# Layer norm of a macaron layer: statistics of the next tile ahead of the current one's finish, loads moved behind it

## The chip, the cores and the metric

The program runs on all 8 cores of one Trainium2 chip. Each core does its own share and none waits for another. The metric is the time on the device of the slowest core, in microseconds (us).

## The reference, cut to what matters

```python
# x: (4, 4096, 2048) float32
x = x + 0.5 * ffn(layernorm(x))     # 2048 -> 8192 -> 2048, 8-bit weights with scales
x = x + attn(layernorm(x))          # chunked gated linear attention
x = x + 0.5 * ffn(layernorm(x))     # the same weights again

def layernorm(x, eps=1e-5):         # over the 2048 features, no gain or bias
    m = mean(x, -1); v = var(x, -1)
    return (x - m) / sqrt(v + eps)
```

## The kernel before, in words

A core owns 2048 rows (tokens) of x and takes 256 rows ahead of them as a prefix: 2304 rows, 18 tiles of 128 rows. The phases follow one another with barriers between them: layer norm 1 with the gate and up products (pG), the down product (pD), layer norm 2 with the key, query and gate products (pKq, pWg), the scan, the output products (pGo), layer norm 3 with gate and up again (16 tiles), and the down product.

All three layer norms are one Python generator in `ln_transpose`, which emits one tile per step. In this text a tile's number is `ti`, and its steps are:

- **Load.** `xload(ti)` issues one DMA of 1 MiB from ScalarE's queue (ACT) into one of two buffers lnx, `ti % 2`. It must wait until the tile two before it in that buffer has been read by the square and by the normalization.
- **Statistics.** VectorE (DVE) sums the tile (L261); ACT squares it with a running sum, L263. The squares themselves are thrown away; they land in the buffer lnxn of that tile, of which there are three (two in layer norm 2).
- **Finish.** Three small DVE operations (L267, L270, L273) make mean and variance, two small ACT operations (Ln L277, Exp L281) the inverse root, one more small one (L284) the offset, and L287 writes the normalized tile in bf16 to lnxn.
- **Transpose.** TensorE (PE) transposes 16 blocks in two halves (L297); ACT copies the first half out of PSUM (L303), DVE the second (L309). In layer norm 2 the tile is also written to HBM (xn2tok) by a DMA from GpSimd's queue (POOL).

In the code before, step `ti` is: issue load `ti + 1`, statistics of `ti`, finish of `ti`, transpose of `ti`. Load 0 is issued when the generator is made, ahead of everything else in the phase.

Every engine runs its instructions in the order in which they were emitted, and a DMA issued from ACT stands in ACT's order like any other instruction. Semaphore waits are put in by a helper that knows the last writer and the readers of each buffer.

The steps are drawn in groups by `drive`: four tiles, then the products that need these 512 rows, then the next four. With 18 tiles the groups are 4, 4, 4, 4 and 2, with 16 tiles four of 4. In the feed-forward phases a group is followed by ten products (five gate, five up blocks) whose evacuations are ACT's Silu (L405) and a DVE operation (L411). Before the first group, ten weight blocks (wraw) are loaded by SyncE's queue (SP) and converted on ACT (L375). In layer norm 2 a group is followed by the key product, and after the third and fifth group also by query products, softmax and the pWg pass; its first group comes right after the issue of four loads of s_wqk from POOL's queue.

Of the kernel before, what the change touches and what calls it, by code (L numbers as in the profile page):

```python
# [11 lines left out]
AF = mybir.ActivationFunctionType  # L12
ALU = mybir.AluOpType
AX = mybir.AxisListType
# [147 lines left out]
def uname(base):  # L162
    _uid[0] += 1
    return f"{base}_{_uid[0]}"


def build_program(T_OWN, T_PRE, stop=99, scan_stop=99):
# [35 lines left out]
    with ExitStack() as ctx:  # L203
        em = Em(nc, ctx)
# [17 lines left out]
        def ln_transpose(al, srcs, xnT, bxnT, TT_loc, tok_dst=None,  # L222
                         nxn=3):
            if True:
                a2 = al
                pT = [a2(nc.psum_tensor(uname("pT"), [128, 1024], BF16))
                      for _ in range(2)]
                bpT = [Buf(uname("bpT"), excl=True) for _ in range(2)]
                s_x = [a2(nc.sbuf_tensor(uname("lnx"), [128, H], F32))
                       for _ in range(2)]  # L230
                s_xn = [a2(nc.sbuf_tensor(uname("lnxn"), [128, H], BF16))
                        for _ in range(nxn)]
                s_st = a2(nc.sbuf_tensor(uname("lnst"), [128, 24], F32))
                bx = [Buf("lnx0"), Buf("lnx1")]
                bxn = [Buf(uname("lnxn")) for _ in range(3)]
                bstl = [Buf(uname("lnst")) for _ in range(3)]
                bsql = [Buf(uname("lnsq")) for _ in range(3)]
                xnT3 = xnT[:, :].rearrange("p (h t) -> p h t", t=TT_loc)
                tiles = []
                for (src, row0, ntiles) in srcs:  # L240
                    for kk in range(ntiles):
                        tiles.append(src[row0 + kk * 128: row0 + (kk + 1) * 128, :])

                def xload(ti):
                    em.dma("dA", s_x[ti % 2][:, :], tiles[ti],
                           writes=[bx[ti % 2]])

                xload(0)

                def _gen():  # L250
                    for ti in range(len(tiles)):
                        sl = ti % nxn
                        c0 = sl * 8
                        X, BX = s_x[ti % 2], bx[ti % 2]
                        XN, BXN = s_xn[sl], bxn[sl]
                        bst = bstl[sl]
                        st = s_st[:, c0:c0 + 8]
                        if ti + 1 < len(tiles):
                            xload(ti + 1)
                        bsq = bsql[sl]  # L260
                        em.op("dve", lambda v: v.reduce_sum(  # L261
                            st[:, 0:1], X[:, :], AX.X), reads=[BX], writes=[bst])
                        em.op("act", lambda a: a.activation(  # L263
                            XN[:, :], X[:, :], AF.Square,
                            accum_out=st[:, 1:2]),
                            reads=[BX], writes=[BXN, bsq])
                        em.op("dve", lambda v: v.tensor_scalar(  # L267
                            st[:, 2:3], st[:, 0:1], 1.0 / H, None, ALU.mult),
                            reads=[bst], writes=[bst])
                        em.op("dve", lambda v: v.tensor_tensor(  # L270
                            st[:, 3:4], st[:, 2:3], st[:, 2:3], ALU.mult),
                            reads=[bst], writes=[bst])
                        em.op("dve", lambda v: v.scalar_tensor_tensor(  # L273
                            st[:, 4:5], st[:, 1:2], 1.0 / H, st[:, 3:4],
                            ALU.mult, ALU.subtract), reads=[bst, bsq],
                            writes=[bst])
                        em.op("act", lambda a: a.activation(  # L277
                            st[:, 5:6], st[:, 4:5], AF.Ln,
                            bias=s_cst[:, 0:1]),
                            reads=[bst, b_c], writes=[bst])  # L280
                        em.op("act", lambda a: a.activation(  # L281
                            st[:, 6:7], st[:, 5:6], AF.Exp, scale=-0.5),
                            reads=[bst], writes=[bst])
                        em.op("dve", lambda v: v.scalar_tensor_tensor(  # L284
                            st[:, 7:8], st[:, 2:3], -1.0, st[:, 6:7],
                            ALU.mult, ALU.mult), reads=[bst], writes=[bst])
                        em.op("dve", lambda v: v.tensor_scalar(  # L287
                            XN[:, :], X[:, :], st[:, 6:7], st[:, 7:8],
                            ALU.mult, ALU.add), reads=[BX, bst], writes=[BXN])
                        if tok_dst is not None:  # L290
                            em.dma("dV", tok_dst[ti], XN[:, :], reads=[BXN])
                        for half in range(2):
                            pb = bpT[half]
                            em.dep_wait("pe", [BXN, b_c], [pb])
                            for hh in range(8):
                                hc = half * 8 + hh
                                ins = nc.tensor.transpose(  # L297
                                    pT[half][:, hh * 128:(hh + 1) * 128],
                                    XN[:, hc * 128:(hc + 1) * 128], s_ident[:, :])
                                if hh == 7:  # L300
                                    em._finish(ins, "pe", 1, [BXN, b_c], [pb])
                            if half == 0:
                                em.op("act", lambda a, ti=ti: a.activation(  # L303
                                    xnT3[:, 0:8, ti * 128:(ti + 1) * 128],
                                    pT[0][:, :].rearrange(
                                        "p (h t) -> p h t", t=128),
                                    AF.Copy), reads=[pb], writes=[bxnT[ti]])
                            else:
                                em.op("dve", lambda v, ti=ti: v.tensor_copy(  # L309
                                    xnT3[:, 8:16, ti * 128:(ti + 1) * 128],  # L310
                                    pT[1][:, :].rearrange(
                                        "p (h t) -> p h t", t=128)),
                                    reads=[pb], writes=[bxnT[ti]])
                        yield ti
                return _gen()

        def drive(gen, done, need):
# [256 lines left out]
        with ExitStack() as ph:  # L574
            alP = ph.enter_context
            xnT = alP(nc.sbuf_tensor("xn1T", [128, NH * TT], BF16))
            bxnT = [Buf(f"xn1T{i}") for i in range(nT)]
            ln_srcs = ([(dx_pre, 0, nPre)] if nPre else []) + [(dx_own, 0, nTo)]
            g_ln = ln_transpose(alP, ln_srcs, xnT, bxnT, TT)
            if stop <= 1:  # L580
                drain(g_ln)
                em.drain_dmas()
                return nc
            ffn_gu(alP, xnT, bxnT, TT, True, ln_gen=g_ln)
# [11 lines left out]
        with ExitStack() as ph:  # L596
# [18 lines left out]
            with ExitStack() as ps:  # L615
                a2 = ps.enter_context
                g_ln = ln_transpose(a2, [(dx1, 0, nT)], xnT, bxnT, TT,
                                    tok_dst=dxn2, nxn=2)
                if stop <= 4:
# [23 lines left out]
                for wi, wsrc_ap in enumerate((dwq, dwk)):  # L643
                    w3 = wsrc_ap.rearrange("(h p) d -> p h d", p=128)
                    for part in range(2):
# [5 lines left out]
                               writes=[b_wqk])  # L651
# [88 lines left out]
                for ng, (o, wd) in enumerate(groups):  # L740
# [5 lines left out]
                        reads=[pbuf], writes=[b_kf])  # L746
# [19 lines left out]
            with ExitStack() as ps:  # L766
# [235 lines left out]
                for po in range(nTo):  # L1002
                    sl = po % 2
# [6 lines left out]
                    for dvc in range(NH):  # L1010
# [9 lines left out]
                        reads=[bpR, b_c], writes=[b_rr])  # L1020
# [3 lines left out]
                        reads=[b_rr], writes=[b_rr])  # L1024
# [8 lines left out]
            for cc in range(NH):  # L1033
                em.dma("dV", s_wo[:, cc * H:(cc + 1) * H], dwbfa[2, cc],
                       writes=[b_wo])
            with ExitStack() as ps:
# [4 lines left out]
                for (o, wd) in tgroups(T_OWN):  # L1041
# [3 lines left out]
                        writes=[b_pGo[0]])  # L1045
                    em.op("dve", lambda v, o=o, wd=wd: v.tensor_copy(
                        s_rb[:, o:o + wd], pGo[:, 0:wd]),
                        reads=[b_pGo[0]], writes=[b_rb])
# [20 lines left out]
                for c in range(T_OWN // SW):  # L1069
                    for cb in range(NH):  # L1070
# [3 lines left out]
                        for g2 in range(SW // 512):  # L1074
# [3 lines left out]
                                   writes=[b_gwi[slw]])  # L1078
                        g0 = (2 * cb) % 4
                        for g2 in range(SW // 512):  # L1080
# [14 lines left out]
                              reads=gbk + [b_gwi[slw]],  # L1095
                              writes=[b_gof])
                        em.op("act", lambda a: a.activation(
                            s_sg[:, 0:SW], s_gof[:, 0:SW], AF.Silu),
                            reads=[b_gof], writes=[b_sg])
# [8 lines left out]
                              reads=[b_o, b_rb, b_c], writes=[b_gof])  # L1108
# [3 lines left out]
                            reads=[b_gof, b_sg], writes=[b_yb])  # L1112
                    for sub in range(SW // 128):
# [3 lines left out]
                               writes=[b_xr2])  # L1117
                        for half in range(2):
                            bk = [b_pGo[2 * half], b_pGo[2 * half + 1]]
                            em.dep_wait("pe", [b_yb, b_wo], bk)  # L1120
                            for cc in range(NH):
                                for tg in range(2):
# [18 lines left out]
                                  reads=bk + [b_xr2], writes=[b_xo2])  # L1141
# [89 lines left out]
```

How the kernel before makes its waits and increments, by code:

```python
    def _wait(self, ename, sem_name, val):  # L56
        if val <= 0:
            return
        w = self.waited[ename]
        if w.get(sem_name, 0) >= val:
            return
        self.eng[ename].wait_ge(self.sem[sem_name], val)
        w[sem_name] = val
# [19 lines left out]
    def _finish(self, ins, sem_name, inc, reads, writes):  # L83
        ins.then_inc(self.sem[sem_name], inc)
        self.cnt[sem_name] += inc
        tag = (sem_name, self.cnt[sem_name])
        for b in writes:
            b.last_w = tag
            b.readers = []
        for b in reads:
            b.readers.append(tag)
        return ins
```

## Time and profile before

| what | value |
|---|---|
| median of three runs | 7669.69 us (7666.61 to 7678.71) |
| the profiled execution: its time / its span | 7678.08 us / 7676.6 us |
| spans of the eight cores | 7647.7 to 7676.6 us |
| PE matmul busy | 6659.8 us (87%) |
| ACT busy / DVE busy / POOL busy | 1545.2 (20%) / 1142.9 (15%) / 281.3 us (4%) |
| DMA engines, mean rate | 83 GB/s |
| layer norm tiles per core | 52 (18 + 18 + 16) |

The profile is of the slowest core, core 3. Its span runs from its first to its last instruction. A bracket at the end of a line of the timeline gives how long the engine had been idle, and what ended that; ACTq, SPq and POOLq are the issues of DMAs from that engine. The granted clock is the share of TensorE's full clock that it was given.

### The profile page before, as it was taken

Reading aid. Unit: us, or ns where it says so; the run is one execution under the profiler, and the core shown is the slowest. Engines: PE = TensorE matmul, PEld = TensorE weight load, DVE = VectorE, ACT = ScalarE, POOL = GpSimd, SP = SyncE. Lnnn points to the kernel's source line nnn. Section 1 sums busy time; section 2 is a strip of 40 time slices with the busy share of each in tenths; the row PEclk is TensorE's granted clock in tenths of the full one; section 3 lists DMA queues with packets and bytes.
Section 4 is the critical chain, followed back from the end, with each engine's and each line's share of the span. In section 5 each row is a group of like instructions: output and inputs, shape, how many; then the busy total and the mean of one; then the engine's idle time right before and its main releaser. Section 6 shows DMA issues by size and latency. Waiting matters only on the chain.

```text
span 7676.6 us, 80477 instructions; the slowest of 8 cores (7647.7 to 7676.6 us)
## 1 busy us (share of the span) xinstructions
PE 6659.8 (87%) x32377; PEld 3176.0 (41%) x32377; DVE 1142.9 (15%) x1540; ACT 1545.2 (20%) x1518; POOL 281.3 (4%) x366
## 2 busy tenths in 40 slices
PE   4599999999978989966656995599999999889899
PEld 1245555555543434433334342244444444334344
DVE  2211111111100000022143331211111111000000
ACT  2232222222221020012223002222222222210200
POOL 0000000000000000000000000000000000000000
PEclk8799999999999999977877997799999999999999
DMA  2133333222124444442212433111111111144444
GB/s 67 44 88 90 85 91 85 85 90 83 38 55 132 115 124 115 115 126 97 101 53 66 137 116 99 55 42 38 38 39 39 39 39 39 55 132 115 125 114 107
DMA packets 743465, 635.59 MB, mean 83 GB/s; under 512 B 581952, under 2 KB 623040, under 8 KB 730048
## 3 DMA queue, kind: packets, MB, share of 16 engines
q10 hardware_dynamic: 590208, 257.98, 12.8%
q1 hardware_dynamic: 102304, 196.28, 8.5%
q0 software_dynamic: 50592, 176.18, 7.8%
q8 instruction: 267, 4.37, 0.2%
q14 instruction: 94, 0.77, 0.0%
HBM read 464.69 MB, written 166.72 MB: 82 GB/s over the span
## 4 chain that ended last, share of the span: by engine, by line
PE 84%; DVE 5%; ACT 5%; DMA 3%; issue 3%; DVEq 0%; ACTq 0%; SPq 0%; POOL 0%; POOLq 0%
PE pG L127 50%; PE pD L545 24%; PE pWg L127 3%; PE pGo L1123 3%; ACT wdsb L524 2%; PE pGo L127 2%; DVE lnst L261 1%; DMA gwi<-gwig 1%; DVE lnxn L287 1%; PE pT L297 1%; PE pKq L127 1%; DVE s_S L968 1%; ACT silu L405 0%; PE pOs L916 0%; DVE hsb L411 0%
## 5 line engine op out<-in xcount | busy, mean ns | idle before, releaser
L545 PE MATMUL pD<-wdsb,hts 128*128 128x512 bf16 x8704 | 1889.0, 380 | 203.7 <-DMA hts<-h4s 203.7
L127 PE MATMUL pG<-xn1T,wbf 128*128 128x512 bf16 (+1 forms) x10240 | 2014.7, 360 | 49.8 <-ACT silu L405 23.9
L127 PE MATMUL pG<-xn3T,wbf 128*128 128x512 bf16 x8192 | 1789.5, 381 | 47.9 <-ACT silu L405 23.7
L127 PEld LDWEIGHTS pG<-xn1T,wbf 128*128 128x128 bf16 x10240 | 1003.4, 98 | 1060.1 <-issue 87.3
L545 PEld LDWEIGHTS pD<-wdsb,hts 128*128 128x128 bf16 x8704 | 853.7, 98 | 1238.8 <-issue 218.4
L127 PEld LDWEIGHTS pG<-xn3T,wbf 128*128 128x128 bf16 x8192 | 802.5, 98 | 1034.0 <-issue 85.4
L405 ACT ACTIVATE silu<-pG,s_gs 128x512 bf16<-128x512 f32 (+1 forms) x576 | 382.1, 663 | 2879.8 <-PE pG L127 2879.7
L411 DVE SCALAR_TENSOR_TENSOR hsb<-pG,s_us,silu 128x512 bf16<-128x512 f32 (+1 forms) x576 | 415.4, 721 | 3484.9 <-PE pG L127 3479.3
L375 ACT ACTIVATE wbf<-wraw 128x2048 bf16<-128x2048 uint8 x256 | 478.8, 1899 | 140.9 <-DMA wraw<-wg 139.1
L297 PE MATMUL pT<-s_ident,lnxn 128*128 128x128 bf16 x832 | 97.0, 310 | 469.8 <-DVE lnxn L287 469.8
L524 ACT ACTIVATE wdsb<-wdu 128x8192 bf16<-128x8192 uint8 x32 | 222.0, 7015 | 961.5 <-issue 900.8
L560 DVE TENSOR_TENSOR t<-pD,dsbl 128x1024 f32<-128x1024 f32 x68 | 83.3, 1225 | 1913.6 <-PE pD L545 1913.6
L113 POOL DMA_DIRECT2D h4s<-hsb x128 | 152.6, 1192 | 4104.8 <-DVE hsb L411 4104.8
L297 PEld LDWEIGHTS pT<-s_ident,lnxn 128*128 128x128 bf16 x832 | 84.7, 144 | 484.8 <-issue 484.8
L1123 PE MATMUL pGo<-s_wo,s_yb 128*128 128x512 bf16 x1024 | 224.1, 382 | 15.8 <-DVE s_yb L1109 15.4
L127 PE MATMUL pGo<-s_o,s_wb 128*128 128x512 bf16 x1024 | 226.4, 383 | 10.4 <-DVE s_gof L1091 9.3
L127 PE MATMUL pWg<-xn2T,wigb 128*128 128x512 bf16 x1024 | 226.1, 385 | 0.0
L263 ACT ACTIVATE lnxn<-lnx 128x2048 bf16<-128x2048 f32 x52 | 98.9, 1902 | 521.1 <-DMA lnx<-x1s 512.5
L1123 PEld LDWEIGHTS pGo<-s_wo,s_yb 128*128 128x128 bf16 x1024 | 100.6, 98 | 139.4 <-issue 20.9
L127 PEld LDWEIGHTS pGo<-s_o,s_wb 128*128 128x128 bf16 x1024 | 100.3, 99 | 137.4 <-issue 21.0
L127 PEld LDWEIGHTS pWg<-xn2T,wigb 128*128 128x128 bf16 x1024 | 101.3, 99 | 124.1 <-issue 6.3
L261 DVE TENSOR_REDUCE lnst<-lnx 128x1 f32<-128x2048 f32 x52 | 118.3, 2276 | 28.3 <-DMA lnx<-x2s 14.4
(110 smaller groups left out, 1564.2 us busy)
## 6 DMA issues: line engine op xcount, KB each, us to landing
hts<-h4s ACTq DMA_DIRECT2D x272, 512.0 KB, 3.9
h4s<-hsb POOLq DMA_DIRECT2D x64, 576.0 KB, 5.4
wraw<-wg SPq DMA_DIRECT2D x128, 256.0 KB, 2.6
wraw<-wu SPq DMA_DIRECT2D x128, 256.0 KB, 2.7
wdu<-wd SPq DMA_DIRECT2D x32, 1024.0 KB, 5.3
h4s<-hsb POOLq DMA_DIRECT2D x64, 512.0 KB, 4.8
wbfa<-cab POOLq DMA_DIRECT2D x48, 512.0 KB, 5.5
x1s<-xo POOLq DMA_DIRECT2D x36, 512.0 KB, 3.8
```

The lines of the kernel that those rows point to most:

```text
L113: ins = self.eng[ename].dma_start(out_ap, in_ap)
L127: ins = self.nc.tensor.matmul(out_ap, l, r, start=(k == 0), stop=last)
L261: em.op("dve", lambda v: v.reduce_sum(st[:, 0:1], X[:, :], AX.X), reads=[BX], writes=[bst])
L263: em.op("act", lambda a: a.activation(XN[:, :], X[:, :], AF.Square, accum_out=st[:, 1:2]), reads=[BX], writes=[BXN, bsq])
L297: ins = nc.tensor.transpose(pT[half][:, hh * 128:(hh + 1) * 128], XN[:, hc * 128:(hc + 1) * 128], s_ident[:, :])
L375: em.op("act", lambda a: a.activation(WB[:, :], WR[:, :], AF.Copy, bias=-128.0), reads=[BWR], writes=[BWB])
L405: em.op("act", lambda a: a.activation(SL[:, o:o + wd], pap, AF.Silu, scale=scale2[:, ib:ib + 1]), reads=[pbuf, b_c], writes=[BSL])
L411: em.op("dve", lambda v: v.scalar_tensor_tensor(HT[:, o:o + wd], pap, scale2[:, ib:ib + 1], SL[:, o:o + wd], ALU.mult, ALU.mult), reads=[p ...
L524: em.op("act", lambda a, c8=c8: a.activation(s_wd[:, c8 * 8 * HH:(c8 + 1) * 8 * HH], s_wdu8[c8 % 2][:, :], AF.Copy, bias=-128.0), reads=[b ...
L545: last_ins = nc.tensor.matmul(pD[sl][:, tg * 512:(tg + 1) * 512], HB[:, il * 128:(il + 1) * 128], s_wd[:, ic * HH + tg * 512: ic * HH + (t ...
L560: em.op("dve", lambda v, sl=sl, half=half: v.tensor_tensor(s_t1[sl][:, :], pD[sl][:, :], s_dsb[:, half * HH:(half + 1) * HH], ALU.mult), r ...
L1123: ins = nc.tensor.matmul(pGo[:, half * 1024 + tg * 512: half * 1024 + (tg + 1) * 512], s_yb[:, cc * SW + sub * 128: cc * SW + sub * 128 + ...
```

## The change

Inside the generator the statistics of a tile become a function `head`, and the order changes. Loads 0 and 1 and the statistics of tile 0 are emitted at the generator's first step, no longer when it is made. Step `ti` then is: statistics of `ti + 1`, finish of `ti`, transpose of `ti`, issue of load `ti + 2`. Buffers, their number, and the work done stay as they were.

```diff
-                xload(0)
+                def head(tj):
+                    slh = tj % nxn
+                    sth = s_st[:, slh * 8:slh * 8 + 8]
+                    Xh, BXh = s_x[tj % 2], bx[tj % 2]
+                    XNh, BXNh = s_xn[slh], bxn[slh]
+                    em.op("dve", lambda v: v.reduce_sum(
+                        sth[:, 0:1], Xh[:, :], AX.X), reads=[BXh],
+                        writes=[bstl[slh]])
+                    em.op("act", lambda a: a.activation(
+                        XNh[:, :], Xh[:, :], AF.Square,
+                        accum_out=sth[:, 1:2]),
+                        reads=[BXh], writes=[BXNh, bsql[slh]])
 
                 def _gen():
+                    xload(0)
+                    if len(tiles) > 1:
+                        xload(1)
+                    head(0)
                     for ti in range(len(tiles)):
...
                         if ti + 1 < len(tiles):
-                            xload(ti + 1)
-                        bsq = bsql[sl]
-                        em.op("dve", lambda v: v.reduce_sum(
-                            st[:, 0:1], X[:, :], AX.X), reads=[BX], writes=[bst])
-                        em.op("act", lambda a: a.activation(
-                            XN[:, :], X[:, :], AF.Square,
-                            accum_out=st[:, 1:2]),
-                            reads=[BX], writes=[BXN, bsq])
+                            head(ti + 1)
...
+                        if ti + 2 < len(tiles):
+                            xload(ti + 2)
                         yield ti
```

## Rows read from the trace of the kernel before

**Rows 1.** The page: chain that ended last by line, and the transposes' group.
```profile
PE pG L127 50%; PE pD L545 24%; PE pWg L127 3%; PE pGo L1123 3%; ACT wdsb L524 2%; PE pGo L127 2%; DVE lnst L261 1%; DMA gwi<-gwig 1%; DVE lnxn L287 1%; PE pT L297 1%; PE pKq L127 1%; DVE s_S L968 1%; ACT silu L405 0%; PE pOs L916 0%; DVE hsb L411 0%
...
L297 PE MATMUL pT<-s_ident,lnxn 128*128 128x128 bf16 x832 | 97.0, 310 | 469.8 <-DVE lnxn L287 469.8
```

**Rows 2.** Windows: length, busy us of PE, PEld, DVE, ACT, POOL, PE clock, DMA.
```profile
122.00:163.00 41.00, 11.15 (x81) 8.12 (x82) 20.20 (x29) 14.99 (x22) 0.00 (x0) 0.61 0.29 103
```

**Rows 3.** Timeline, two neighbouring tiles of layer norm 1: start, us, instruction [idle before].
```profile
52.71 1.35 DVE L287 TENSOR_SCALAR lnxn<-lnx,lnst 128x2048 bf16<-128x2048 f32 x1
...
54.42 1.87 PE L297 MATMUL pT<-s_ident,lnxn 128*128 128x128 bf16 x16 [6.87 <-DVE lnxn L287]
...
55.60 0.34 ACTq L113 DMA_DIRECT2D lnx<-x_own  x1
...
56.65 0.69 DVE L309 COPY xn1T<-pT 128x1024 bf16<-128x1024 bf16 x1 [2.60 <-ACT xn1T L303]
57.26 2.27 DVE L261 TENSOR_REDUCE lnst<-lnx 128x1 f32<-128x2048 f32 x1
...
60.48 0.29 ACT L277 ACTIVATE lnst<-lnst,s_cst 128x1 f32<-128x1 f32 x1 [2.05 <-DVE lnst L273]
...
61.44 1.35 DVE L287 TENSOR_SCALAR lnxn<-lnx,lnst 128x2048 bf16<-128x2048 f32 x1
```

**Rows 4.** DMA issues of lnx by stretch: count, KB, median us to landing; last, all 52.
```profile
lnx<-x_own ACTq DMA_DIRECT2D x13, 1024.0 KB, 5.0
...
lnx<-x1s ACTq DMA_DIRECT2D x13, 1024.0 KB, 5.5
...
lnx<-x2s ACTq DMA_DIRECT2D x14, 1024.0 KB, 4.8
...
lnx<-x1s ACTq DMA_DIRECT2D x1, 1024.0 KB, 7.7
...
DMA to landing us min/median/max: 4.7/5.2/12.1
```

**Rows 5.** DMA issues at the program's start; the load is the second one.
```profile
s_ident<-ident SPq DMA_DIRECT2D x1, 32.0 KB, 4.6
...
s_gs<-gs SPq DMA_DIRECT2D x1, 32.0 KB, 1.8
...
lnx<-x_pre ACTq DMA_DIRECT2D x1, 1024.0 KB, 6.6
```

**Rows 6.** Timeline, layer norm 1: issue of load 1, normalization of tile 0.
```profile
39.08 0.34 ACTq L113 DMA_DIRECT2D lnx<-x_pre  x1
...
44.19 1.35 DVE L287 TENSOR_SCALAR lnxn<-lnx,lnst 128x2048 bf16<-128x2048 f32 x1
```

**Rows 7.** Timeline, layer norm 2: writes 0 and 1, square 2, key product.
```profile
3403.46 1.10 POOL L113 DMA_DIRECT2D xn2tok<-lnxn  x2
...
3410.93 1.91 ACT L263 ACTIVATE lnxn<-lnx 128x2048 bf16<-128x2048 f32 x1 [8.55 <-DMA xn2tok<-lnxn]
...
3427.75 5.54 PE L127 MATMUL pKq<-xn2T,s_wqk 128*128 128x512 bf16 x16 [1.21 <-DVE xn2T L309]
```

**Rows 8.** Timeline, layer norm 3: issues of loads 0 and 1, normalization of tile 0.
```profile
4669.32 0.36 ACTq L113 DMA_DIRECT2D lnx<-x2s  x1
...
4699.65 0.33 ACTq L113 DMA_DIRECT2D lnx<-x2s  x1
...
4706.04 1.35 DVE L287 TENSOR_SCALAR lnxn<-lnx,lnst 128x2048 bf16<-128x2048 f32 x1
```

**Rows 9.** DMA issues of wraw: the first of phase 3, then all 128.
```profile
wraw<-wg SPq DMA_DIRECT2D x1, 256.0 KB, 7.1
...
wraw<-wg SPq DMA_DIRECT2D x128, 256.0 KB, 2.6
```

**Rows 10.** The chain in order of time: first product after two of the groups.
```profile
251.27 6.58 PE pG L127 x16
...
339.81 5.00 PE pG L127 x16
```

More of the change, by code:

```diff
@@ L257, in _gen @@
                         st = s_st[:, c0:c0 + 8]
+                        bsq = bsql[sl]
                         if ti + 1 < len(tiles):
-                            xload(ti + 1)
-                        bsq = bsql[sl]
-                        em.op("dve", lambda v: v.reduce_sum(
-                            st[:, 0:1], X[:, :], AX.X), reads=[BX], writes=[bst])
-                        em.op("act", lambda a: a.activation(
-                            XN[:, :], X[:, :], AF.Square,
-                            accum_out=st[:, 1:2]),
-                            reads=[BX], writes=[BXN, bsq])
+                            head(ti + 1)
                         em.op("dve", lambda v: v.tensor_scalar(
```

## The prediction, on record before the result

> **What bounds the kernel now.** I read the page's shares and chain first. The chain is PE nearly throughout, and the layer norm has three entries of about 1% in it, the sum L261, the normalization L287 and the transposes [rows 1]. The transposes' row says more: PE sat idle 469.8 us ahead of them, 9.0 us for each of 52 tiles, every time ended by L287 [rows 1]. So the layer norm is exposed, tile by tile, and nothing else runs on PE meanwhile: in the stretch of the second group PE is busy 11.15 us of 41, most of that products at its two ends [rows 2]. What one tile takes longer, the kernel takes longer.
>
> The timeline of two neighbouring tiles gives the cycle [rows 3]. L287 starts at 52.71 and again at 61.44: a period of 8.73 us. Within it, counted from the end of L287 at 54.06: PE starts at +0.36, the next load is issued at +1.54, DVE copies its half at +2.59, and the next sum starts at +3.20. From the start of the sum to the next L287 it is 4.18 us. The load is not in this loop: the one issued at +1.54 is for the tile after the next, so it has 1.66 us plus a whole period, 10.4 us, before anyone reads it, and it takes 4.8 to 5.5 us [rows 4].
>
> **The change, part by part.**
>
> *Statistics one tile ahead: nothing gained in the middle.* DVE runs in order. Before, its order is sum(i), small ones(i), L287(i), copy(i), sum(i+1). After, it is sum(i+1), small ones(i), L287(i), copy(i), sum(i+2). There is still one full sum between copy and the next small ones, so it covers none of DVE's idle gaps (2.60 us ahead of the copy [rows 3]). ACT's square lies beside the sum as before. Price and gain: 0 per tile. Only a layer norm's last tile has no statistics in its step: 2.27 us saved [rows 3], three times: -6.8.
>
> *The load behind the finish: its cover is gone.* Load i+2 is issued at the end of step i, which is the same point of the cycle as before, +1.54. But the next instruction on both DVE and ACT is now the statistics of this very tile i+2, and the finish of tile i+1, whose data are long there, is queued behind them on both engines; PE waits for that finish. So the sum starts at +1.54, plus the landing, plus 0.1 for the wait to pass (my allowance), in place of +3.20. With the medians of the three layer norms [rows 4]:
> - layer norm 1: 1.54 + 5.0 + 0.1 - 3.20 = 3.44 us more per stall;
> - layer norm 2: with 5.5, 3.94 us;
> - layer norm 3: with 4.8, 3.24 us.
>
> To hide the load it would have to land within 1.56 us; the fastest of all 52 took 4.7 [rows 4].
>
> *How many stalls.* The load issued at a group's end flies during the products, so the group's first step does not wait. The other three steps of a group of four do, also the fourth, which takes the statistics of the next group's first tile before its own finish. The last group's last step has no statistics, and a group of two has no stall. That makes 3+3+3+3+0 = 12 for layer norm 1, as many for layer norm 2, and 3+3+3+2 = 11 for layer norm 3.
> - Layer norm 1: 12 x 3.44 = 41.3.
> - Layer norm 2 without its first group: 9 x 3.94 = 35.5.
> - Layer norm 3: 11 x 3.24 = 35.6.
> Together 112.4 us for 32 stalls. Bounds: with 4.7 for each, 32 x 3.14 = 100; with 7.7 (the slowest load late in layer norm 2 [rows 4]) for the nine of layer norm 2 and 5.4, my guess from the medians, for the others, 9 x 6.14 + 23 x 3.84 = 144.
>
> The Trainium skill, page "DMA: Bandwidth & Descriptors", section on the anatomy of one DMA, puts a transfer at about 2.0 us plus bytes over 436 GB/s, fitted for DMAs issued by GpSimd. For 1 MiB that is 4.4 us, an estimate; by it a stall would be 2.8 us and the 32 of them 91 us. The trace has 4.7 to 5.5 for loads issued by ACT in the steady part, so the sum goes by the trace. By the page too, the fixed 2.0 us alone exceed the room there is.
>
> *First group of layer norm 2.* There the third tile already waits: square 2 overwrites lnxn 0, whose write to HBM stands on POOL's queue behind the s_wqk loads, is issued at 3403.46, and lets the square go at 3410.93 [rows 7]. From there to the key product it is 16.8 us. After the change the same square stands ahead of the finish of tile 1. The later start of tile 0 is hidden in this wait. From the square: 2.1 us of it and its accumulator read, 1.0 from Ln to L287(1) [rows 3], then two stalled periods of 8.73 + 3.94 = 12.67, then 4.8 from L287(3) to the product (16.8 less 8.73 and less the 3.3 from square to L287): 33.2 us, 16.4 more. The write may land up to 2.4 us sooner when it no longer shares with write 1, so 14.0 to 16.4; I take 15.5.
>
> *The starts.* In layer norm 1 load 0 is now issued behind the ten conversions, with load 1 right behind it, where load 1 is issued today at 39.08 [rows 6]. That place took 6.6 us for one load [rows 5]; a second one behind it lands, I estimate, 3.7 later: less than the 4.7 of the fastest load, since what is fixed in a load overlaps. (Where two are issued together now, in layer norm 2, the second takes 12.1 [rows 4].) Sum 1 then starts at 39.1 + 10.4 = 49.5, and L287 of tile 0 at 53.7 instead of 44.19: +9.5. Against it, load 0 no longer competes with the small constants at the front: s_ident took 4.6 us, s_gs of the same size 1.8 [rows 5], and each waits for the one before it and the weights for all of them. I credit 2.5 of at most some 3.4: +7.0. In layer norm 3 the first wraw took 7.1 us beside load 0 and 2.6 otherwise [rows 8, 9], so the conversions move up by at most 4.5; I take 4.0. Loads 0 and 1 then go at 4695.7, the second lands about 9.2 later, L287 follows 4.2 after the sum's start and 1.3 for the table load that Ln needs there: 4710.5 against 4706.04 [rows 8], +4.5. Both starts +11.5, between +6 and +18.
>
> *The clock.* The layer norms run at the low clock already, 0.61 granted over that stretch [rows 2], so longer gaps have little left to take. The first product after a group takes 6.58 us in some and 5.00 in others [rows 10]. Of the eight such products with 512 columns in the two feed-forward phases six are like the first of these rows, each with a second slow product behind it, and the difference over both is 3.3 us. A new draw could give back 20 or cost 7; I take 0.
>
> *Sum:* 112.4 + 15.5 + 11.5 - 6.8 = +132.6 us. Against the profiled execution's own time, 7678.1, that is 7810.7; it lies 8.4 above the median of the runs shown, so against the median, which I forecast, 7802.
>
> **Rivals.**
> - *The sum comes out of the loop* (ends on the other side). Statistics a tile ahead are to take 2.3 us off each tile. It holds if DVE finds the sum ready to run in its idle gap; 49 x 2.4 = -118 us, 7552. DVE's 2.60 us gap speaks for it. In-order issue behind the load of the same tile speaks against it, and it decides only if loads land within 1.56 us.
> - *No change.* The stall is just hidden, at a landing near 1.6 us: 7670. All 52 landings speak against it.
> - *Partly hidden.* Some finishes slip through, or half of the stalls in a group are shorter since the queue is emptier: about half the stalls, 7745. For it: layer norm 2 has other waits already. Against it: the layer norms have nothing else on the queues in phases 1 and 3.
> - *Dearer.* Loads on the path see contention or the clock costs after every group: 32 stalls at 6.1 instead of 3.5, +216 in all, 7886. Only the load late in layer norm 2 speaks for it.
>
> **How the numbers follow.** The forecast's case gets 0.83, partly hidden 0.07, dearer 0.05, faster 0.03, no change 0.02. Its range, all ends low: 100 + 14 + 6 - 7 - 20 = +93, all high: 144 + 16 + 18 - 7 + 7 = +178. I take 7768 to 7848 as the range. A change under 0.2%, 15 us, is about what a measurement of this kernel cannot tell from none. Faster 0.03, same 0.02, slower 0.95.
>
> **What would show it.** In the profile after: a period near 12.2 us within a group and 8.7 for its first tile; the sum L261 and the square L263 in 35 places with an idle time ended by the DMA of lnx, 3 to 4 us beyond what they idle now; PE's idle time before the transposes near 600 us instead of 469.8; s_ident landing in about 2 us; the products as they were. The prediction is wrong if sums start right behind the copies, or if loads land in clearly less than 4.7 or more than 6 us.

## The result, and the profile after

The changed kernel takes 1.0166 times as long as before (95% interval 1.0150 to 1.0182): 7669.7 becomes some 7797 us, +127. The prediction was 7802. Some executions leave the four cores of a die, or all eight, at a lower granted clock (down to 0.78, where the others have 0.925 to 0.94) and take longer, so where an experiment is compared below, its number is the mean span of the cores over those dies alone whose granted clock lies within 0.004 of the highest of that kernel: 7660 us for the kernel before (single dies 7656 to 7667), 7784 for the changed one (7780 to 7800), +124.

The page of the changed kernel, first from the costliest groups (busy, mean ns of one, idle before and its releaser), then the DMA issues with their median us to landing, over the whole execution:

```profile
L306 PE MATMUL pT<-s_ident,lnxn 128*128 128x128 bf16 x832 | 97.0, 309 | 586.8 <-DVE lnxn L296 586.8
...
L253 DVE TENSOR_REDUCE lnst<-lnx 128x1 f32<-128x2048 f32 x52 | 118.8, 2284 | 220.4 <-DMA lnx<-x1s 72.8
```
```profile
lnx<-x1s ACTq DMA_DIRECT2D x18, 1024.0 KB, 5.4
lnx<-x_own ACTq DMA_DIRECT2D x16, 1024.0 KB, 4.9
lnx<-x2s ACTq DMA_DIRECT2D x16, 1024.0 KB, 4.8
...
s_ident<-ident SPq DMA_DIRECT2D x1, 32.0 KB, 2.7
```

PE's idle time ahead of the transposes grew from 469.8 [rows 1] to 586.8 us, by 117, which is nearly all of the loss. The loads themselves land as before (4.8 to 5.4 against 4.8 to 5.5 [rows 4]); they are only waited for now. The timeline of two neighbouring tiles of layer norm 1, to be laid beside [rows 3], shows where (L296 is the normalization that was L287, L253 the sum that was L261, L256 the square, L318 DVE's copy):

```profile
63.14 1.35 DVE L296 TENSOR_SCALAR lnxn<-lnx,lnst 128x2048 bf16<-128x2048 f32 x1
64.85 1.87 PE L306 MATMUL pT<-s_ident,lnxn 128*128 128x128 bf16 x16 [9.91 <-DVE lnxn L296]
...
66.03 0.33 ACTq L113 DMA_DIRECT2D lnx<-x_own  x1
67.09 0.69 DVE L318 COPY xn1T<-pT 128x1024 bf16<-128x1024 bf16 x1 [2.60 <-ACT xn1T L312]
70.92 1.91 ACT L256 ACTIVATE lnxn<-lnx 128x2048 bf16<-128x2048 f32 x1 [3.94 <-DMA lnx<-x_own]
70.93 2.29 DVE L253 TENSOR_REDUCE lnst<-lnx 128x1 f32<-128x2048 f32 x1 [3.15 <-DMA lnx<-x_own]
...
75.17 1.35 DVE L296 TENSOR_SCALAR lnxn<-lnx,lnst 128x2048 bf16<-128x2048 f32 x1
```

Up to the copy the cycle is the same to a hundredth: the load is issued 1.54 us after L296's end, the copy starts at 2.60. Then DVE and ACT idle until the load issued a moment ago has landed, 4.9 us after its issue. The square that ends this wait belongs to the tile after the next; the tile whose transposes PE is waiting for had its data all along. L296 to L296 is 12.03 us here instead of 8.73.

The stages, as means over the eight cores of one profiled execution (layer norms 1 and 2 with the products among their groups; the third from the end of pWg to its last copy). In that of the changed kernel cores 4 to 7 took 15 us more than cores 0 to 3 (7800.1 against 7785.3), so its row is some 7 us high:

| kernel | LN 1 | FFN 1 | LN 2 | scan, pGo, LN 3 | FFN 2 | all |
|---|---|---|---|---|---|---|
| before | 402.0 | 2967.4 | 497.5 | 1116.9 | 2678.2 | 7662.1 |
| changed | 448.4 | 2968.2 | 539.4 | 1154.2 | 2682.6 | 7792.7 |
| statistics in place, load late | 443.9 | 2968.2 | 545.6 | 1154.8 | 2676.7 | 7789.2 |
| changed, three lnx buffers in LN 1 and 3 | 402.7 | 2967.4 | 539.7 | 1117.4 | 2679.7 | 7707.0 |
| changed, loads 0 and 1 early | 442.3 | 2967.6 | 539.7 | 1149.6 | 2677.9 | 7777.0 |
| statistics in the gaps, ACT's queue | 366.6 | 2968.2 | 476.4 | 1085.2 | 2679.6 | 7576.0 |

### The profile page after: what moved, and what is told of

It reads as the page before. It is cut to its first block, busy times and chain, and to the rows that moved or that the text cites. A ratio compares the mean times of both kernels' runs of the same rounds, so it can differ in the third digit from the quotient of the medians.

```text
span 7810.0 us, 80408 instructions; the slowest of 8 cores (7773.6 to 7810.0 us)
## 1 busy us (share of the span) xinstructions
PE 6669.3 (85%) x32377; PEld 3178.2 (41%) x32377; DVE 1142.0 (15%) x1540; ACT 1550.1 (20%) x1518; POOL 280.4 (4%) x366
## 4 chain that ended last, share of the span: by engine, by line
PE 82%; DMA 6%; DVE 5%; ACT 4%; issue 3%; DVEq 0%; ACTq 0%; POOL 0%; SPq 0%; POOLq 0%
PE pG L127 49%; PE pD L556 24%; PE pGo L1134 3%; PE pWg L127 3%; ACT wdsb L535 2%; PE pGo L127 2%; DVE lnst L253 1%; DMA gwi<-gwig 1%; DVE lnxn L296 1%; DMA lnx<-x1s 1%; DMA lnx<-x_own 1%; DMA lnx<-x2s 1%; PE pT L306 1%; DMA wdu<-wd 1%; DVE s_S L979 1%
## 5 line engine op out<-in xcount | busy, mean ns | idle before, releaser
L306 PE MATMUL pT<-s_ident,lnxn 128*128 128x128 bf16 x832 | 97.0, 309 | 586.8 <-DVE lnxn L296 586.8
L256 ACT ACTIVATE lnxn<-lnx 128x2048 bf16<-128x2048 f32 x52 | 99.2, 1907 | 682.8 <-DMA lnx<-x1s 562.9
L253 DVE TENSOR_REDUCE lnst<-lnx 128x1 f32<-128x2048 f32 x52 | 118.8, 2284 | 220.4 <-DMA lnx<-x1s 72.8
```

The costliest lines, as they stand in the source:

```text
L253: em.op("dve", lambda v: v.reduce_sum(sth[:, 0:1], Xh[:, :], AX.X), reads=[BXh], writes=[bstl[slh]])
L256: em.op("act", lambda a: a.activation(XNh[:, :], Xh[:, :], AF.Square, accum_out=sth[:, 1:2]), reads=[BXh], writes=[BXNh, bsql[slh]])
L306: ins = nc.tensor.transpose(pT[half][:, hh * 128:(hh + 1) * 128], XN[:, hc * 128:(hc + 1) * 128], s_ident[:, :])
```

## The experiments

**The late load alone.** The order of the statistics is that of the kernel before; only the load moves.

```diff
-                        if ti + 1 < len(tiles):
-                            xload(ti + 1)
                         bsq = bsql[sl]
...
+                        if ti + 1 < len(tiles):
+                            xload(ti + 1)
                         yield ti
```

> The kernel before with one thing changed: the load of tile i+1 is issued at the end of step i instead of at its start; statistics stay in their old place. Theory (the price is a load whose landing the in-order engines wait for): the period within a group goes from 8.73 to about 12.0 us, in 13 + 12 places of layer norms 1 and 3 and 9 or 10 of layer norm 2 plus its first group; 35 x 3.3 = 115, with the first group some +120 us in all, ratio 1.015 to 1.017. Rival (the statistics ahead of the finish are what costs): the order of DVE and ACT work is that of before, so within 0.2% of before.

Measured: 7792 us, +132, slightly more than the change itself. There is no later start of layer norm 1 in it (tile 0 is normalized at 43.9 us in the mean of the eight cores, before at 43.7), but each layer norm's last step is stalled too: 11.8, 14.4 and 11.9 us where the kernel before has 8.5, 8.7 and 8.7. From its timeline in layer norm 1 (L285 is the normalization, L261 the square):

```profile
57.62 1.35 DVE L285 TENSOR_SCALAR lnxn<-lnx,lnst 128x2048 bf16<-128x2048 f32 x1
59.33 1.86 PE L295 MATMUL pT<-s_ident,lnxn 128*128 128x128 bf16 x16 [11.21 <-DVE lnxn L285]
...
60.45 0.33 ACTq L113 DMA_DIRECT2D lnx<-x_own  x1
...
65.73 1.91 ACT L261 ACTIVATE lnxn<-lnx 128x2048 bf16<-128x2048 f32 x1 [4.27 <-DMA lnx<-x_own]
...
69.94 1.35 DVE L285 TENSOR_SCALAR lnxn<-lnx,lnst 128x2048 bf16<-128x2048 f32 x1
```

The period is 12.32 us with the statistics where they were. So a load issued just ahead of the first instruction that reads it reproduces the loss, and taking the statistics ahead is not needed for it. The rival that blames the order of the statistics falls: with the old order it said no change, within 0.2%.

**The wait removed by a third buffer.** In layer norms 1 and 3 the load of tile i+2 goes at the start of step i into a third lnx buffer. It takes the place of the third lnxn. Layer norm 2, which has only two lnxn, stays as changed and serves as a control.

```diff
-                         nxn=3):
+                         nxn=2):
...
+                nx = 2 if tok_dst is not None else 3
...
+                        if nx == 3 and ti + 2 < len(tiles):
+                            xload(ti + 2)
                         if ti + 1 < len(tiles):
                             head(ti + 1)
...
-                        if ti + 2 < len(tiles):
+                        if nx == 2 and ti + 2 < len(tiles):
                             xload(ti + 2)
                         yield ti
```

> The changed kernel with a third lnx buffer in layer norms 1 and 3 (in exchange two lnxn buffers instead of three), so that each load is issued a whole period before its statistics; layer norm 2 stays as in the changed kernel. Theory: in layer norms 1 and 3 the period is 8.7 us or a little less (8.5), and of the some 84 us that these two cost in the change only the later starts remain, about 5; layer norm 2 keeps its 42 us. In all +35 to +50 us against before, ratio 1.005 to 1.0065. Rival (statistics ahead cost by themselves): stays at +120 to +130 us. Rival (they gain once the load is early): layer norms 1 and 3 come out over 20 us faster than before.

Measured: 7707 us, +47. The stage table has the split: layer norm 1 is back to 402.7 us (before: 402.0), the third stage to 1117.4 (1116.9), and layer norm 2 keeps its 42 us. From the timeline of layer norm 1 (L299 normalizes, L254 sums):

```profile
60.65 1.35 DVE L299 TENSOR_SCALAR lnxn<-lnx,lnst 128x2048 bf16<-128x2048 f32 x1
62.36 1.86 PE L309 MATMUL pT<-s_ident,lnxn 128*128 128x128 bf16 x16 [6.61 <-DVE lnxn L299]
...
65.20 2.28 DVE L254 TENSOR_REDUCE lnst<-lnx 128x1 f32<-128x2048 f32 x1
...
69.12 1.35 DVE L299 TENSOR_SCALAR lnxn<-lnx,lnst 128x2048 bf16<-128x2048 f32 x1
```

The period is 8.47 us, 0.26 under that of before, with no wait for a DMA ahead of the sum. The order of the change is harmless once the loads are early, and all but worthless: 0.26 us a tile, and one sum less at the end of each layer norm, which the later starts take back (in layer norm 1 tile 0 is normalized 7.4 us later than before, as the mean of the eight cores). The third lnxn went at the same time; that its loss costs nothing is seen only in this sum.

**Half the bytes.** Every load brings the first 1024 columns alone; the other half of each buffer holds a constant, so the output is that of other data.

```diff
-                    em.dma("dA", s_x[ti % 2][:, :], tiles[ti],
+                    em.dma("dA", s_x[ti % 2][:, 0:H // 2],
+                           tiles[ti][:, 0:H // 2],
```

> The changed kernel where each load brings only the first 1024 of the 2048 columns; the other half of the buffers holds a constant, so the normalization works on data that are half left out. All compute instructions stay. Theory: a stall shrinks by what the landing shrinks, from 4.9 to about 3.2 us (the 512 KB writes and loads land in 3.2 to 3.4), so by 1.7 us in 35 places, 60 us, and a few us at the starts: +60 to +75 us against before, ratio 1.008 to 1.010. Rival (the cost is in the order of instructions, not in the bytes): stays near +127 us.

Measured: 7742 us, +82, 42 less than the changed kernel. The direction is that of the theory, the size was missed: I had taken 3.2 us for the landing of 512 KB. The kernel before already had a nearer row, loads of 512 KB from ACT's queue (hts<-h4s, 272 of them) with a median of 3.9 us. On core 0:

```profile
DMA to landing us min/median/max: 3.5/4.0/7.4
```
```profile
142.42 0.33 ACTq L113 DMA_DIRECT2D lnx<-x_own  x1
143.47 0.69 DVE L323 COPY xn1T<-pT 128x1024 bf16<-128x1024 bf16 x1 [2.38 <-ACT xn1T L317]
146.22 1.91 ACT L261 ACTIVATE lnxn<-lnx 128x2048 bf16<-128x2048 f32 x1 [2.85 <-DMA lnx<-x_own]
146.23 2.29 DVE L258 TENSOR_REDUCE lnst<-lnx 128x1 f32<-128x2048 f32 x1 [2.06 <-DMA lnx<-x_own]
```

The sum starts 3.81 us after the issue in place of 4.90, 1.1 us sooner, and 35 x 1.1 is 38 of the 42 us; layer norm 1 also starts some 2 us sooner. That the data differ is not what helps: on cores 0 to 3 the two feed-forward phases take 2 and 3 us more than in the changed kernel, and the stages with the layer norms 18, 14 and 14 less. The price follows the landing time, and that shrinks much less than by half: with medians of 4.0 and 5.1 us, and taken as linear, 2 x 4.0 - 5.1 = 2.9 us of a load do not depend on its bytes, an estimate. The Trainium skill, page "DMA: Bandwidth & Descriptors", section on the anatomy of one DMA, has that shape: it would give 3.2 us for half a load and 4.4 for a whole one, as estimates. The trace has medians of 4.0 and 4.8 to 5.4 for these loads from ACT's queue.

**The first loads early.**

```diff
+                xload(0)
+                if len(tiles) > 1:
+                    xload(1)
+
                 def _gen():
-                    xload(0)
-                    if len(tiles) > 1:
-                        xload(1)
                     head(0)
```

> The changed kernel with loads 0 and 1 issued when the generator is made, ahead of the conversions, as load 0 was before. Theory: only the starts change. Tile 0 of layer norm 1 is normalized at about 46 us instead of 51.6, in layer norm 3 about 2.5 us sooner, and all stalls stay: 8 us faster than the changed kernel, ratio to before 1.0155. Rival (the starts are a large part of the loss): over 30 us faster than the changed kernel.

Measured: 7783 us, 1 less than the changed kernel where I expected 8, between dies that differ by some 20: no difference that these runs can tell. The two loads now stand in the way of the constants, and the weights behind them (in the changed kernel s_umask took 1.7 us, and the first weights were issued at 11.14 us; here at 16.62):

```profile
s_umask<-umask SPq DMA_DIRECT2D x1, 64.0 KB, 6.9
s_ident<-ident SPq DMA_DIRECT2D x1, 32.0 KB, 3.0
```

Tile 0 of layer norm 1 is normalized at 48.52 us in place of 51.59, 3 us sooner where I expected 5.5. The rival with the starts as a large part is out: they are worth a few us, and the stalls stay (the periods within the first group are 11.60, 12.17 and 11.79 us).

**Statistics in the gaps.** This asks whether the next tile's statistics can be made to pay. The square is emitted behind Exp, the sum behind the normalization, and the load behind the sum, all ahead of the transposes and copies. Loads 0 and 1 are where the kernel before has them. In the edit hsq is the square and hsum the sum.

```diff
                             st[:, 6:7], st[:, 5:6], AF.Exp, scale=-0.5),
                             reads=[bst], writes=[bst])
+                        if ti + 1 < len(tiles):
+                            hsq(ti + 1)
...
                             ALU.mult, ALU.add), reads=[BX, bst], writes=[BXN])
+                        if ti + 1 < len(tiles):
+                            hsum(ti + 1)
+                        if ti + 2 < len(tiles):
+                            xload(ti + 2)
```

> Statistics of the next tile again, but placed in the idle gaps: the square right behind Exp of the current tile on ACT, the sum right behind the normalization on DVE, where it idles 2.6 us for the transposes; the load of tile i+2 right behind the normalization of tile i, ahead of ACT's copy. Loads 0 and 1 are issued where the kernel before has them. Theory (only what stands in a gap leaves the loop, and only if its load has landed): the sum's 2.3 us leave the period, 8.73 to about 6.5 us; a load has some 5 us from issue to its square and takes 4.8 to 5.5, so the square waits up to 1 us but still ends about when the copy can start. Some 50 tiles x 2.2 = 110 us faster than before, ratio 0.984 to 0.988. Rival (any statistics ahead wait for their load, which becomes the new bound): the period stays above 8 us, within 20 us of before.

Measured: 7576 us, 83 less than before (ratio of the two means 0.989) and 208 less than the changed kernel. Its profiled execution took 7585 us, where that of the kernel before took 7678. From the timeline of layer norm 1 (L303 normalizes, L252 sums, L261 squares, L329 copies):

```profile
50.49 1.35 DVE L303 TENSOR_SCALAR lnxn<-lnx,lnst 128x2048 bf16<-128x2048 f32 x1
...
51.75 2.28 DVE L252 TENSOR_REDUCE lnst<-lnx 128x1 f32<-128x2048 f32 x1
51.91 0.33 ACTq L113 DMA_DIRECT2D lnx<-x_own  x1
52.20 1.86 PE L317 MATMUL pT<-s_ident,lnxn 128*128 128x128 bf16 x16 [4.80 <-DVE lnxn L303]
...
54.43 0.69 DVE L329 COPY xn1T<-pT 128x1024 bf16<-128x1024 bf16 x1 [0.41 <-ACT xn1T L323]
...
56.65 1.91 ACT L261 ACTIVATE lnxn<-lnx 128x2048 bf16<-128x2048 f32 x1 [0.26 <-DMA lnx<-x_own]
56.76 1.35 DVE L303 TENSOR_SCALAR lnxn<-lnx,lnst 128x2048 bf16<-128x2048 f32 x1
```

The sum fills DVE's wait for the transposes, of which 0.41 us is left, and the period is 6.27 us. The square still waits 0.26 us for its load, beside the normalization, at no cost. Layer norms 1 and 3 give 35 and 32 us, layer norm 2 only 21, and this is where most of the 110 us that I expected went missing. Its first group gives nothing (52.4 us from the first load to the product, before 51.2, means of the eight cores), and ACT's squares wait there for the writes to HBM of the tile whose lnxn they overwrite.

```profile
DMA xn2tok<-lnxn: 37.5, 8
```

That row, from the waits of lnx's instructions on ACT and DVE, has 37.5 us in 8 places; the kernel before had one such wait, of 8.55 us [rows 7]. That this wait is the cause is read from the trace; no run gives layer norm 2 a third lnxn.

**The same with SP's queue.**

```diff
-                    em.dma("dA", s_x[ti % 2][:, :], tiles[ti],
+                    em.dma("dS", s_x[ti % 2][:, :], tiles[ti],
```

> The same as the kernel with statistics in the gaps, but the loads of lnx are issued from SP's queue instead of ACT's, so that a load neither waits for ACT to reach it nor stands ahead of ACT's copy. Theory: the load goes at the end of the normalization plus 0.1 in place of plus 0.5, the square is not waited for; 0 to 0.4 us less per tile, so 0 to 20 us faster than with ACT's queue, ratio to before 0.982 to 0.987. Rival (SP's own weight loads get in the way): slower than with ACT's queue at the starts of the phases.

Measured: 7575 us, 1 less than with ACT's queue: the same. With the load this early, the issuing queue makes no difference that these runs can tell; the 0 to 20 us I had allowed come out at the low end.

## Why the prediction was right

Step by step, from the profiled executions; the slowest cores are core 3 before and core 7 after:

| step | predicted | slowest core of each | mean of the eight cores |
|---|---|---|---|
| 12 stalls of layer norm 1 | +41.3 | +41.2 | +37.9 |
| 9 of layer norm 2 | +35.5 | +33.4 | +34.0 |
| 11 of layer norm 3 | +35.6 | +32.5 | +34.0 |
| first group of layer norm 2 (first load to product) | +15.5 | +12.3 | +13.8 |
| start of layer norm 1 | +7.0 | +7.4 | +6.9 |
| start of layer norm 3 (first wraw to L296) | +4.5 | +1.8 | +4.4 |
| the three last tiles | -6.8 | -7.0 | -7.0 |
| distances between the groups, layer norm 2 | 0 | -3.3 | -2.9 |
| sum | +132.6 | +118 | +121 |

The cause and nearly all of the amount are the predicted ones, and the sum was some 12 us too high. The measured +124 to +127 holds a few us beside these terms: on cores 0 to 3 of the changed kernel alone they sum to 122 of the 123 us by which those cores exceed the mean before. Cores 4 to 7 lost their 15 us more in stretches of products, core 7 itself 23 us behind its last normalization, where the change touches nothing.

- *Where the stalls are.* Right in number and place. The periods of layer norm 1 are 11.55, 12.03, 11.81 in the first group, then 12.55, 11.71, 11.84 and so on; the last is 6.42, with no statistics in its step.
- *Their size.* The wait was sized rightly: from the issue of a load to the sum it is 5.05, 5.75 and 5.01 us in the three layer norms, means of the eight cores over the stalls, where I had 5.1, 5.6 and 4.9. But the small operations no longer follow upon the sum that they read, and from the sum's start to the normalization it is 3.93 us in 32 of the 52 tiles where it was 4.19 (the tile shown above, with 4.24, is an exception). That the period of the three-buffer kernel is 8.47 has the same 0.26 in it. I had put the price of the new order at 0 per tile; 32 x 0.26 is 8 us, and the stalls came to 105.9 instead of 112.4. That core 7 has 41.2 against the 41.3 predicted is luck: the eight cores have 35.9 to 41.2.
- *The first group of layer norm 2.* The mechanism held as described; write 0 still goes out behind the s_wqk loads and gates square 2:

```profile
3416.74 0.82 ACTq L113 DMA_DIRECT2D lnx<-x1s  x2
...
3441.79 0.56 POOL L113 DMA_DIRECT2D xn2tok<-lnxn  x1
...
3448.14 1.91 ACT L256 ACTIVATE lnxn<-lnx 128x2048 bf16<-128x2048 f32 x1 [12.09 <-DMA xn2tok<-lnxn]
...
3481.33 5.31 PE L127 MATMUL pKq<-xn2T,s_wqk 128*128 128x512 bf16 x16 [1.21 <-DVE xn2T L318]
```

From the square to the product it is 33.19 us; I had worked out 33.2. The 2.4 us by which the write might land sooner came from no row; the trace has 2.2 of them: the square goes 6.0 us after the write's issue where it went after 8.2 (means of the eight cores), with write 1 issued 10.8 us behind write 0 and no longer 0.55. So the low end, 14.0, was the right one.

- *The starts.* s_ident lands in 2.7 us in place of 4.6 [rows 5], and the loads of layer norm 1 are issued 3.2 us earlier for it (35.85 against 39.08 [rows 6]), 0.7 more than the credit of 2.5. The first of them landed 8.2 us after its issue on this core, where I had taken 6.6 (the eight cores have 5.5 to 9.0), and the second 3.5 us behind it, where I had guessed 3.7. The errors nearly cancel:

```profile
35.85 0.90 ACTq L113 DMA_DIRECT2D lnx<-x_pre  x2
...
44.07 2.29 DVE L253 TENSOR_REDUCE lnst<-lnx 128x1 f32<-128x2048 f32 x1 [30.66 <-DMA lnx<-x_pre]
47.58 2.29 DVE L253 TENSOR_REDUCE lnst<-lnx 128x1 f32<-128x2048 f32 x1 [1.22 <-DMA lnx<-x_pre]
...
51.59 1.35 DVE L296 TENSOR_SCALAR lnxn<-lnx,lnst 128x2048 bf16<-128x2048 f32 x1
```

- *The clock.* The seven distances between groups of 512 columns in the two feed-forward phases hold 59 to 62.5 us each on most cores, and which ones hold 62 changes from core to core. On the two slowest cores they sum to 10 us less after the change, over the eight cores to 4.5 us more (cores 4 and 5 have four of 66 to 69 us), on cores 0 to 3 to 1.5 us more than the mean before. So 0 was near, within a few us; what single distances do is a draw that no run here explains.
- *The rivals.* The sum can leave the loop, as the rival that ends faster had it, but only in another place of the queue; as the change has it, it is behind the load. "Partly hidden" and "dearer" had nothing for them in the trace: all 32 stalls are there, at 3.1 to 3.8 us each as the mean of a layer norm.
- *Slips that cost nothing.* In the stretch of the second group PE is busy 11.15 us, but 7.46 of them are the 64 transposes and only 3.69 products, not most of it products as I read it. And the low end of the range does not follow from its own sum: 7669.7 + 93 is 7763, not 7768.

## What to carry to other kernels

Look at what is queued behind a wait, on every engine: here the finish of a tile whose data were there waited for a load for another tile. Work taken ahead paid here only in a place where its engine idles and its data have landed; count the distance from the issue of the load to its first reader, in the new order, before moving either. With two buffers a load can't be issued before the second last tile is done with, so the reader has to be put late in the step, or a third buffer found.

## What the runs showed that was not expected

- Three small DVE operations behind an independent sum instead of their own: 3.93 in place of 4.19 us from the sum's start to the normalization, in 32 of the 52 tiles. That their reading of a just written value costs this is argued, not shown.
- A load of half the bytes, 512 KB instead of 1 MiB, took 4.0 us in the median against 5.1 over all 52 of the changed kernel.
